# Eight feature tiles of batch 0 multiplied at the end of stage one, and expert_w applied to the latents

## The reference, cut to what matters

```
x = LN(x + attention(x))                # attention over 8 key/value groups inside each token
x = LN(x + fake_quant(x) @ fake_quant(ctx))        # ctx: 2 x 1024 x 1024
x = LN(x + ffn(x))

ffn(x):  r = sum(top_2(x @ gate_w))                # 8 columns, one number per token
         h = relu(x @ up_w) ** 2                   # up_w 1024 x 2048
         latent = x @ fc1_w                        # fc1_w 1024 x 512
         expert = latent @ expert_w                # expert_w 512 x 512
         return LN(h @ down_w + (expert * r) @ fc2_w) * gamma + beta
```

## Time and profile before

| | us |
|---|---|
| median of three runs | 710.58 (708.35 to 712.87) |
| the profiled execution | 706.96 |
| its span on the core | 705.2 |
| TensorE busy in the span | 620.1 (88%) |
| VectorE, ScalarE, GpSimd busy | 415.0, 292.9, 137.9 |
| last cross product of stage one begins | 241.73 |
| first matmul of the feed-forward part | 253.62 |
| last matmul of its first products / first of its seven phases | about 490 / 493.4 |

### The profile page before, as it was taken

The page is one execution under the profiler, slowest core; times in us unless marked ns, Lnnn a source line. Parts: engine busy times, 40 slices in busy tenths (PEclk is TensorE's granted clock), DMA queues, the critical chain, the costliest instruction groups (busy, mean ns, idle before and its releaser), DMA issues.

```text
span 705.2 us, 7841 instructions
## 1 busy us (share of the span) xinstructions
PE 620.1 (88%) x2952; PEld 501.4 (71%) x2960; DVE 415.0 (59%) x552; ACT 292.9 (42%) x378; POOL 137.9 (20%) x162
## 2 busy tenths in 40 slices
PE   4598699887559879989999999998999999999972
PEld 3487577765348548868888888886888888888862
DVE  6846788997888523222334222132875555769976
ACT  4545555556363524222233323203254433434825
POOL 3424283555730411313110000000000000000000
PEclk9999999998878999999999999999999999999987
DMA  9654335433761469684884825500433235352402
GB/s 337 226 170 152 112 108 169 131 92 102 244 198 39 145 203 316 207 293 149 263 304 149 273 107 158 171 8 1 122 113 94 89 91 201 126 210 61 148 31 119
DMA packets 80887, 109.88 MB, mean 156 GB/s; under 512 B 23633, under 2 KB 54609, under 8 KB 80849
## 3 DMA queue, kind: packets, MB, share of 16 engines
q1 hardware_dynamic: 76096, 92.07, 40.6%
q0 software_dynamic: 2448, 8.91, 3.6%
q10 hardware_dynamic: 2304, 8.39, 3.5%
HBM read 79.99 MB, written 25.17 MB: 149 GB/s over the span
## 4 chain that ended last, share of the span: by engine, by line
PE 58%; DVE 21%; DMA 7%; issue 5%; ACT 4%; SPq 4%; POOL 2%; POOLq 0%; DVEq 0%; ACTq 0%
PE acc_b L1172 31%; PE acc_a L1201 13%; PE acc_b L1201 8%; DMA c_sb<-in_ctx_dram 2%; SPq L243 1%; SPq L235 1%; DVE stat L571 1%; DMA x_scratch<-res 1%; PE qkv_ps L283 1%; PE sc_ps L300 1%; DVE o_sb L615 1%; ACT y_sb L425 1%; DVE x2T_hi L1457 1%; PE xa_ps L325 1%; DVE stat_n L1508 1%
## 5 line engine op out<-in xcount | busy, mean ns | idle before, releaser
L1388 DVE TENSOR_TENSOR u_lo<-u_raw,u_hi 128x1024 fp32r<-128x1024 f32 x18 | 23.3, 1293 | 123.1 <-ACT u_hi L1244 123.1
L1172 PE MATMUL acc_b<-x2T_hi,u_hi 128*128 128x512 f32 x160 | 63.3, 396 | 0.0
L1172 PE MATMUL acc_b<-x1T_hi,u_hi 128*128 128x512 f32 x160 | 62.4, 390 | 0.0
L1172 PE MATMUL acc_b<-x2T_hi,u_lo 128*128 128x512 f32 x160 | 62.4, 390 | 0.0
L1172 PE MATMUL acc_b<-x2T_lo,u_hi 128*128 128x512 f32 x160 | 62.3, 390 | 0.0
L1172 PE MATMUL acc_b<-x1T_hi,u_lo 128*128 128x512 f32 x160 | 62.3, 389 | 0.0
L1172 PE MATMUL acc_b<-x1T_lo,u_hi 128*128 128x512 f32 x160 | 62.3, 389 | 0.0
L283 PE MATMUL qkv_ps<-w_hi,xT_hi 128*128 128x512 f32 (+1 forms) x128 | 35.9, 362 | 14.7 <-DVE w_lo L642 10.0
L1201 PE MATMUL acc_a<-x2T_lo,x2T_hi 128*128 128x512 f32 x168 | 41.8, 404 | 3.8 <-DVE x2T_lo L1459 3.8
L1201 PE MATMUL acc_a<-x1T_hi,x2T_hi 128*128 128x512 f32 x168 | 41.1, 399 | 3.0 <-DVE x1T_hi L1459 3.0
L1201 PEld LDWEIGHTS acc_a<-x2T_lo,x2T_hi 128*128 128x128 f32 x168 | 32.9, 197 | 11.7 <-issue 4.6
(11 more groups left out here) (235 smaller groups left out, 1346.1 us busy)
## 6 DMA issues: line engine op xcount, KB each, us to landing
d_raw<-in_L_ffn_down_w_dram SPq DMA_DIRECT2D x28, 512.0 KB, 5.5
t_scratch<-d_raw SPq DMA_DIRECT2D x20, 512.0 KB, 4.2
d_raw<-t_scratch SPq DMA_DIRECT2D x20, 512.0 KB, 3.8
c_sb<-in_ctx_dram ACTq DMA_DIRECT2D x16, 512.0 KB, 4.7
u_raw<-in_L_ffn_up_w_dram SPq DMA_DIRECT2D x16, 512.0 KB, 6.6
x_sb<-in_x_dram SPq DMA_DIRECT2D x8, 512.0 KB, 4.7
res<-in_x_dram SPq DMA_DIRECT2D x8, 512.0 KB, 3.4
x_scratch<-res SPq DMA_DIRECT2D x8, 512.0 KB, 3.6
```

The costliest lines, as they stand in the source:

```text
L1172: mm = pe.matmul(acc_b[:, q % 4], s, v, start=(k == 0 and i == 0), stop=(k == KT - 1 and i == 2))
L1388: dve.tensor_tensor(u_lo[:, m % 2], u_raw[:, m % 2], u_hi[:, m % 2].bitcast(F32), ALU.subtract).then_inc(S["u_lo_done"], 1)
```

## The change

In stage one, W2 is not computed any more: the loads of expert_w and fc2_w, the 16 transposes, the 96 matmuls, the split copies, the evacuations, the stores and the waits for these stores are gone. In their place the first eight 128-column tiles of up_w (EARLY = 8) are loaded, split and multiplied with batch 0, and relu and square are applied: 8 products of 24 matmuls. All eight slices of batch 0's x2 are now loaded at once and transposed in step 8, ahead of tile 7's scores. In the feed-forward part the first products are those with fc1_w (8 products), then expert_w is applied to the latents (8 products of 12 matmuls) and r after it, and then up_w follows; for its first eight tiles only batch 1's product is left. The seven phases read fc2_w itself. The buffers of h are cut into other parts of memory for this. The lists of the engines for stage one's end, and the diff at its core:

```diff
             def load_xk(k):
...
+                    sp.wait_ge(S["c_done"], BATCH * CK)
+                sp.dma_start(xk[k], x2_dram[0:SEQ, k * P:(k + 1) * P].rearrange("(t p) c -> p t c", p=P)).then_inc(xk_in[k], 16)
+            def load_early(m):
+                if m < 2:
+                    sp.wait_ge(S["xT_ready"], TILES - 1 + m)
+                else:
+                    sp.wait_ge(S["early_lo_done"], m - 1)
+                half, j = m % 2, m // 2
+                src = args["up_w"][:, half * HID // 2 + j * P:half * HID // 2 + (j + 1) * P].rearrange("(k p) c -> p k c", p=P)
+                sp.dma_start(early_raw[:, m % 2], src).then_inc(early_in[m % 2], 16)
...
                 if s == TILES:
-                    for k in range(4):
+                    for k in range(KT):
                         load_xk(k)
+                    for m in range(min(2, EARLY)):
+                        load_early(m)
...
                 if in_range(s - 4):
                     t = s - 4
                     sp.wait_ge(S["x2_done"], t + 1)
                     sp.dma_start(x2_dram[t * P:(t + 1) * P, :], res[:, t % XR]).then_inc(x2_st[t % XR], 16)
-            store_w2(range(MT - 1, MT))
+                if s >= TILES:
+                    for m in range(2 * (s - TILES + 1), min(2 * (s - TILES + 2), EARLY)):
+                        load_early(m)
# TensorE, stage one
+            def early_product(m):
+                if m < 2:
+                    pe.wait_ge(S["qkv_evac"], TILES)
+                    pe.wait_ge(S["x2T_lo_done"], KT)
                 else:
+                    pe.wait_ge(S["early_relu"], m - 1)
+                pe.wait_ge(S["early_lo_done"], m + 1)
+                for k in range(KT):
+                    st = [x[:, m % 2, k] for x in (xT_hi, xT_lo)]
+                    for i, (a, v) in enumerate(split_products(st, (x2T_hi[:, k], x2T_lo[:, k]))):
+                        mm = pe.matmul(qkv_ps[:, m % 2 * BANK:(m % 2 + 1) * BANK], a, v, start=(k == 0 and i == 0), stop=(k == KT - 1 and i == 2))
+                mm.then_inc(S["early_used"], 1)
...
                 if s == TILES:
-                    transpose_expert(0)
-                    transpose_expert(1)
+                    transpose_x2(0)
+                    transpose_x2(1)
                 if in_range(s - 2):
                     values(s - 2)
                 if s == TILES:
+                    for k in range(2, KT):
+                        transpose_x2(k)
+                    if EARLY:
+                        early_product(0)
...
                 if in_range(s - 1):
                     scores(s - 1)
+                if s == TILES and EARLY:
+                    early_product(1)
+                if s == TILES + 1 and EARLY:
+                    early_product(2)
+                    early_product(3)
+                if s == TILES + 2 and EARLY:
+                    early_product(4)
                 if in_range(s - 3):
                     if s >= TILES:
                         transpose_q1(s - 3)
                     cross(s - 3)
-                for q in w2_behind.get(s, ()):
-                    w2_product(q)
+            for m in range(5, EARLY):
+                early_product(m)
# ScalarE, stage one
+            def early_hi(m):
+                act.wait_ge(early_in[m % 2], 16 * (m // 2 + 1))
...
+                act.activation(xT_hi[:, m % 2], early_raw[:, m % 2], ACT.Copy).then_inc(S["early_hi_done"], 1)
...
+            def early_out(m):
+                early_relu(m)
+                if m + 2 < EARLY:
+                    early_hi(m + 2)
+                early_square(m)
...
                 if s == TILES:
                     query_diagonal(s - 1)
+                    x2T_hi_out(0)
+                    x2T_hi_out(1)
+                    for m in range(min(1, EARLY)):
+                        early_hi(m)
+                    for k in range(2, 6):
+                        x2T_hi_out(k)
+                    for m in range(1, min(2, EARLY)):
+                        early_hi(m)
+                if in_range(s - 3):
+                    quantise_a(s - 3)
...
+                    softmax_exp(s - 1)
+                    if EARLY:
+                        early_out(0)
+                if s == TILES + 1 and EARLY:
+                    early_out(2)
+                    early_out(3)
+                if s == TILES + 2 and EARLY:
+                    early_out(4)
                 if in_range(s - 3) and s >= TILES:
                     q1T_out(s - 3)
+                if s == TILES and EARLY:
+                    early_out(1)
...
+            for m in range(5, EARLY):
+                early_out(m)
# VectorE, stage one, step TILES
                 if s == TILES:
                     softmax_transpose(s - 2)
+                    for k in range(4):
+                        x2T_lo_out(k)
                 if s in (TILES, TILES + 1):
                     first_stats(s - 3)
                 if in_range(s - 1):
                     values_transpose(s - 1)
...
+                if s == TILES:
+                    x2T_lo_out(4)
+                    x2T_lo_out(5)
...
                 if s in (TILES, TILES + 1):
                     magic(s - 3)
                 if s == TILES:
+                    for m in range(min(1, EARLY)):
+                        early_lo(m)
+                    x2T_lo_out(6)
+                    x2T_lo_out(7)
                     collect(s - 2)
+                    for m in range(1, min(2, EARLY)):
+                        early_lo(m)
# VectorE, stage one: early_lo(2) and early_lo(3) stand around softmax_transpose(7), early_lo(4) behind magic(6),
# early_lo(5) behind magic(7) and ahead of cross_residual(6), early_lo(6) behind tile 6's second normalisation, early_lo(7) last
# TensorE, feed-forward part
             routing(0)
+            latent_product(0, 0)
+            transpose_logits(0)
+            latent_product(1, 0)
+            latent_product(0, 1)
+            spread_r(0)
+            latent_product(1, 1)
+            routing(1)
+            latent_product(2, 0)
+            transpose_logits(1)
+            latent_product(2, 1)
+            latent_product(3, 0)
+            spread_r(1)
+            latent_product(3, 1)
             for b in range(BATCH):
+                for e in range(MT):
+                    expert_product(e, b)
+            for m in range(MU):
+                if m >= EARLY:
+                    up_product(m, 0)
+                up_product(m, 1)
```

More of the change, by code:

```diff
@@ L47 @@
 MT = LAT // P
+EARLY = 8
 MAGIC = 1.5 * 2.0 ** 23
@@ L91, in attention_and_cross @@
         q1T = sb("q1T", [P, 2, KT, P], BF16)
[L92 to L95, removed]
+        q2 = sb("q2", [P, BATCH, CK, EMB], BF16)
         c_sb = sb("c_sb", [P, 2, EMB], F32)
@@ L138, in attention_and_cross @@
         x2_st = so["x2_st"]
-        xk_in, u_in, gate_in = [sem(f"xk_in{i}") for i in range(4)], so["u_in"], sem("gate_in")
+        xk_in, u_in, gate_in = [sem(f"xk_in{i}") for i in range(KT)], so["u_in"], sem("gate_in")
         names = """xT_ready xT_hi_done xT_lo_done qkv_ready qkv_evac q_bd_done k_bd_done vT_done v_bd_done
@@ L753, in _ @@
                     magic(s - 3)
+                    for m in range(5, min(6, EARLY)):
+                        early_lo(m)
                 if in_range(s - 4):
@@ L805, in _ @@
                 if s == TILES + 2:
+                    for m in range(6, min(7, EARLY)):
+                        early_lo(m)
                     for i in range(2):
                         split_u(i)
+                if s == TILES + 3:
+                    for m in range(7, EARLY):
+                        early_lo(m)
                 if s == -1:
@@ L940, in feed_forward, with two_types, h_pair, h_slot @@
         xT_hi, xT_lo = [so["x2T_hi"], x1_hi], [so["x2T_lo"], x1_lo]
-        f1b0, f2b0, f1b1, f2b1 = [sb(n, [P, NP, SEQ], F32) for n in ("f1b0", "f2b0", "f1b1", "f2b1")]
-        h_block = lambda m, b: ((f1b0, f1b1), (f2b0, f2b1))[m % 2][b][:, m // 2]
+        def two_types(name, slots):
+            with nc.sbuf_tensor(name + "_r", [P, slots, SEQ], F32R) as rounded:
+                pass
+            return rounded, sb(name, [P, slots, SEQ], F32)
+        ex_hi, h_a1 = two_types("h_a1", 4)
+        ex_lo, h_a2 = two_types("h_a2", 4)
+        lat_st, h_b = zip(*[two_types(f"h_b{i}", 4) for i in range(4)])
+        h_c = [sb(f"h_c{i}", [P, 2, SEQ], F32) for i in range(4)]
+        part_of = [(so["hx1"][:, KT:KT + 4], h_b[0], h_c[0]), (so["hx2"][:, KT:KT + 4], h_b[1], h_c[1]), (h_a1, h_b[2], h_c[2]), (h_a2, h_b[3], h_c[3])]
+        def h_pair(half, b, j):
+            part = part_of[2 * b + half][j // 2]
+            return part[:, 2 * (j % 2):2 * (j % 2) + 2]
+        def h_slot(half, b, k):
+            return h_pair(half, b, k // 2)[:, k % 2]
+        lat = [[lat_st[2 * b + l // 2][:, 2 * (l % 2):2 * (l % 2) + 2] for b in range(BATCH)] for l in range(MT)]
         s3_own = sb("s3_own", [P, 2, SEQ], F32)
@@ L946, in feed_forward @@
```

(3 more changed lines are left out.)

448 lines of the change are left out of this document (192 added, 256 removed).

## The result

The changed kernel took 737.5 us (734.4 to 741.0, four runs) against 709.5 us. The ratio is 1.039, 95% interval 1.032 to 1.047: slower, on the forecast side, inside the range of 709 to 738 but at its upper edge, 11.5 us above the 726 forecast and above the 716 to 734 that the forecast gave itself. Its profiled execution took 740.95 us, span 739.2, so it is one of the longer ones; before, 706.96 and 705.2. The difference of the spans, 34.0, is what the two traces have to explain.

A forecast was written before the change was run, and what follows sets the result against it. Matmuls bound the feed-forward part, queue order and loads stage one's end. Stage end +40 and feed-forward -24.8 gave +15.2 on 706.96, so 722.2; at the median's level, 3.6 higher, 725.8, said as 726; range 709 to 738.

The forecast's parts named there:

- the third rival: Feed-forward part: up_w loads take 9.3 us instead of 6.6, making products late, about 10 us, 736 in all; chance 0.12.
- the sign named for that rival: Feed-forward part of the profile after: idle gaps returning between the one-batch products would show the third rival holds.
- Milestones of the stage end: Stage one's end: chained times from tile 7's scores to the first feed-forward matmul at 293.7, +40 us.
- tile 7's scores: Stage one's end: scores at 212, +14 us, as the slices come late and early_product(0), 5.45 us, stands before them.
- tile 7's values: Stage one's end: values 13.8 us after the scores, at 226.2, +13, with cross product 5 coming first.
- tile 5's x2 stored: Stage one's end: tile 5's x2 done 8.5 us after the values ended, at 238.3, +12.
- the lower clock: Stage one's end: TensorE restarting slower after three long waits, up to 2 us each, 6 in all; not counted.
- the two loads and the ScalarE steps behind them: Stage one's end: early up_w loads issued behind x2 stores, their splits ahead of q1T_out, delaying cross products 6 and 7.
- the last stretch: From the last cross product to the feed-forward part: three products 16.4 us, relu and square 1.2, barrier 2.1.
- the feed-forward risk: First eight up_w tiles, one product each: weight loads might land too late; 0 to 10 us, taken as 1.
- The two smaller gains: Feed-forward start: batch 1's slices load sooner, about 1.4 us; the wait before batch 1's routing goes, 2.6 us.

The follow-up runs named there:

- b: Changed kernel with SP issuing the loads of up_w tiles 4 to 7 ahead of its waits for attention output and x2; 724.4 us, ratio 1.022.
- c: Changed kernel with ScalarE doing q1T_out ahead of early_out in steps 9 and 10; 722.2 us, ratio 1.020.
- e: Changed kernel with the edits of b, c and d together; 705.6 us, ratio 0.998 to the kernel before.
- j: As i, with TensorE doing tile 7's scores ahead of early_product(0); 704.1 us, ratio 0.996.
- i: As e, with ScalarE copying slices 2 to 5 of batch 0 before it splits the first up_w tile; 703.0 us, ratio 0.991.
- d: Changed kernel with VectorE splitting up_w tile m+2 before it forms the down_w sums of tile m; 725.4 us, ratio 1.024.
- k: Changed kernel with SP issuing the first five down_w loads one up_w tile sooner; 724.0 us, ratio 1.022.
- a: Changed kernel with EARLY = 0, so no product of batch 0 in stage one, only the feed-forward half left; 727.7 us, ratio 1.027.
- l: As i, with the first five down_w loads issued one up_w tile sooner; 702.4 us, ratio 0.991.

## Why the prediction was right, and where it was off

**The sign and the mechanism** were right. The changed kernel is slower because the early products' loads and splits stand in front of the tile pipeline in SP's and ScalarE's lists. b and c show it from two sides. It is 17.7 of the 31.8 us that e gives back, though; the other 14.1 come from the sums of down_w, which the forecast did not have. The number landed in the range because the range was drawn wide enough for the third rival. It lies outside the forecast's own 716 to 734, and the sign named for that rival, idle gaps between the one-batch products, is what the profile shows.

**Milestones of the stage end**, forecast against the trace less the 3.2 us of spread: tile 7's scores 212 and 213.4; tile 7's values 226.2 and 225.8; tile 5's x2 stored 238.3 and 236.5; cross product 6's end 253.0 and 252.7; tile 6's x2 stored 261.8 and 261.5; cross product 7's end 274.0 and 274.6; first feed-forward matmul 293.7 and 293.6.

**Inside those numbers several things cancel.** I had left out the lower clock, "up to 2 us after each of three long waits". Two of them came: cross products 6 and 7 took 6.4 and 5.0 us instead of 3.4 and 3.6, 4.4 more. Against it, tile 5's x2 came 1.8 earlier than I had it, the two loads and the ScalarE steps behind them took some 1.9 less (the splits began 5.4 and 5.6 us after the stores instead of 6.3 and 5.9), and the last stretch took 19.0 instead of 19.7. So the agreement to 0.1 us at the end is luck: the mechanism is shown by b and c, not by it.

**The step "tile 7's scores"** has the right size and a wrong reason. I let the product ahead of the scores delay the softmax chain and so the values. j put the scores first and the values came no sooner. What counts is when `early_product(0)` can start and how much TensorE work stands between it and the values. The start did depend on ScalarE waiting for the first up_w tile: the wait was 5.4 us, and i, which removes it, gained 2.5. The first tile was there at 197.2, forecast 193.6 and 3.2 of spread. The Trainium skill's rule on 512 B transfers (DMA: Bandwidth & Descriptors, Specifications) would have had it some 3 us sooner; the trace sides with the measured 268 GB/s: from 185 to 197.2 us, where the slices and these tiles load, the changed kernel moved 284 GB/s with the DMA engines full. The 398 GB/s beside it in rows 8 were stores of 4 KB rows, not loads, so these two rows alone do not tell row length from direction.

**The term that was mis-sized** is the feed-forward risk: "bounds 0 to 10 us over the four pairs; I take 1". The part gave back 9.2 instead of 24.8. The chain has 8.9 us of waits for the split (4.75, 0.2 and 3.95), the first and last followed by several us at half clock: 428.3 with the sums behind the split against 442.4 is 14.1 in all. With that gone, d's feed-forward part is 23.3 shorter than before's 451.6, against 24.8 forecast. The two smaller gains came as well: the waits of 1.3 and 2.6 us in the first products before have no counterpart in the changed kernel. My argument looked at the weight tiles' own landing, 6.6 us against a window of 8.4, and that was fine. It did not ask what else VectorE waits for ahead of the split. (Its 3 MB in 10.9 us are 289 GB/s with tiles of 512 KB, not 275; d moved 257 in this stretch and lost nothing.) The third rival had "the weight stream binds as well" with a chance of 0.12 and a price of 10 us. Its price was nearer than the 1 us, but its mechanism, the up_w loads, was not the cause: k and d both remove the loss without touching them.

The remaining 1.5 us lies ahead of the seven phases: 4.8 us of wait (3.1 before). The last product now ends in relu and square on ScalarE, and the first split of the phase follows them there (522.8 us), where a latent's product with r on VectorE stood; no run tests this reading.

**The transposes and the clock.** From 200 to 216 us of the changed kernel, with the last transposes and `early_product(0)`, the granted clock was 0.56 on average, 11.2 of 16 us busy. The Trainium skill (TensorE: Matmul & The Clock Gate, PE-mode transpose) has transposes not count as activity; this trace agrees as far as it goes, but TensorE also waited for VectorE, 4.5 us just ahead of that stretch and 1.0 and 3.8 us in it, so it does not tell the two apart.

**The sum, again, with measured terms**: +3.2 of spread, +40.0 of stage end, -24.8 forecast for the feed-forward part, and +15.6 of it not got back (14.1 of split waits and 1.5 ahead of the seven phases): 34.0.

## What to carry to other kernels

Filling an engine's idle time with work from a later stage is priced by the instructions in front of which its loads, splits and evacuations stand in the other engines' lists: here 43.6 us of matmuls moved forward cost 35.6 us of stage time with one order and 12 to 16 with another (88.9 in i and 92.4 in l, against 76.5 in a). Before moving work into a hole, go through each list and put whatever the critical chain needs ahead of whatever may wait for a load. And when a stream is made twice as fast, check every other wait that stands ahead of its steps, not only the stream's own.

## What the runs showed of the hardware

- With 96 matmuls and 16 transposes taken off a stretch where TensorE was not the bound (a_early0), the stretch was no shorter: the three cross products left in it ran at granted clocks of 0.54 to 0.67 and took 18.0 us together instead of 10.4. In e_all3, where early products stand between them and the waits for loads are gone, two of them took 3.6 us each at 1.00.
- A full-width VectorE split took 3.4 us instead of 1.2 at 390 us in the changed kernel, and a down_w sum 2.8 instead of 0.7 at 379.6, both while GpSimd added beta to x2 (2.4 us of work there each time).
- The end of tile 7's projection, before anything was changed, lay between 158.3 and 165.7 us in the profiled executions; the milestones behind it can only be compared from a common anchor, and even from the end of cross product 4 the same code (i and l) differed by 3.5 us.
